# Idle products on TensorE ahead of ten waits between the stages of an eight-stage flamingo block

## What is computed

```python
x = x + tanh(g_xattn[0]) * mamba(ctx, layernorm(x))           # selective scan, 16 states
x = x + tanh(g_ffn[0])   * moe_sigmoid(layernorm(x))          # 16 experts, top 4, one shared
x = x + tanh(g_xattn[1]) * mamba(ctx, layernorm(x))
x = x + tanh(g_ffn[1])   * ternary_ffn(layernorm(x))          # weights quantised to -1, 0, 1
x = x + tanh(g_xattn[2]) * attention(layernorm(x), ctx)       # 32 heads, rotary positions
x = x + tanh(g_ffn[2])   * fp8_ffn(layernorm(x))
x = x + tanh(g_xattn[3]) * feature_attention(layernorm(x), ctx)
x = x + tanh(g_ffn[3])   * moe_softmax(layernorm(x))          # 16 experts, top 2, shared part
```

## Time and profile before

| | |
|---|---|
| median of 3 runs | 996.89 us (996.51 to 998.3) |
| profiled execution, first to last instruction | 994.6 us |
| PE busy | 824.6 us, 83% |
| DVE busy | 670.0 us, 67% |
| POOL, ACT busy | 419.8 us (42%), 406.1 us (41%) |
| mean granted TensorE clock | 0.893 of full speed |

### The profile page before, as it was taken

The page is one execution under the profiler, slowest core; times in us unless marked ns, Lnnn a source line. Parts: engine busy times, 40 slices in busy tenths (PEclk is TensorE's granted clock), DMA queues, the critical chain, the costliest instruction groups (busy, mean ns, idle before and its releaser), DMA issues.

```text
span 994.6 us, 12963 instructions
## 1 busy us (share of the span) xinstructions
PE 824.6 (83%) x4202; PEld 523.7 (53%) x4202; DVE 670.0 (67%) x1145; ACT 406.1 (41%) x832; POOL 419.8 (42%) x313
## 2 busy tenths in 40 slices
PE   7968898756899888888399779999948988979992
PEld 3323333344677767665377535555525776546651
DVE  5989999697889888889565556778727365412222
ACT  5742333253344444443354725665523432113331
POOL 3036666113575766665169402425501341423331
PEclk9979988756999999999599889999978996979997
DMA  5121214381221221220200121332144010161114
GB/s 216 48 84 67 81 64 181 157 271 52 85 85 50 78 84 42 84 84 0 75 0 1 54 64 50 100 114 76 49 144 135 1 58 7 48 202 48 44 48 153
DMA packets 28531, 81.68 MB, mean 82 GB/s; under 512 B 3360, under 2 KB 17200, under 8 KB 27088
## 3 DMA queue, kind: packets, MB, share of 16 engines
q1 hardware_dynamic: 26080, 73.25, 21.5%
q0 software_dynamic: 2256, 6.18, 1.7%
q10 hardware_dynamic: 144, 1.57, 0.4%
HBM read 65.64 MB, written 17.35 MB: 83 GB/s over the span
## 4 chain that ended last, share of the span: by engine, by line
PE 46%; issue 21%; DVE 17%; POOL 9%; DMA 3%; ACT 2%; SPq 0%; DVEq 0%; POOLq 0%; ACTq 0%
PE ps L522 5%; POOL M L689 5%; PE ps L1357 5%; PE ps L1727 4%; PE ps L1731 4%; PE ps L513 3%; PE ps L1769 3%; PE ps L396 3%; PE ps L911 3%; POOL ZT L994 2%; DVE M L658 2%; PE ps L1376 2%; DVE M L666 2%; PE ps L799 2%; PE ps L1642 1%
## 5 line engine op out<-in xcount | busy, mean ns | idle before, releaser
L799 PE MATMUL ps<-W,F 128*128 128x256 f32 x544 | 151.9, 404 | 34.8 <-DVE W L867 21.7
L799 PEld LDWEIGHTS ps<-W,F 128*128 128x128 f32 x544 | 102.2, 198 | 67.6 <-DVE W L867 40.9
L600 POOL TENSOR_TENSOR M<-M 128x1024 f32<-128x1024 f32 x32 | 75.4, 2356 | 86.1 <-DVE M L474 47.4
L696 POOL TENSOR_TENSOR W<-W,M 128x1024 f32<-128x1024 f32 x32 | 75.4, 2357 | 84.4 <-DVE M L666 84.4
L1798 ACT ACTIVATE N<-ps 128x512 f32<-128x512 f32 x128 | 69.5, 594 | 75.7 <-PE ps L1731 75.7
L831 ACT ACTIVATE F<-ps 128x128 f32<-128x128 f32 x136 | 37.8, 278 | 140.0 <-PE ps L799 140.0
L658 DVE TENSOR_TENSOR_SCAN M<-ps,M 128x512 f32<-128x512 f32 x64 | 78.0, 1219 | 21.5 <-POOL M L689 21.5
L1819 DVE TENSOR_REDUCE W<-ps 128x4 f32<-128x1024 f32 x64 | 78.1, 1221 | 8.9 <-PE ps L1731 5.9
L786 PE MATMUL ps<-W,F 128*128 128x256 f32 x272 | 83.3, 389 | 0.0
L1727 PE MATMUL ps<-M,W 32*128 32x256 f32 x512 | 74.1, 418 | 10.8 <-DVE W L1825 5.7
L616 DVE TENSOR_TENSOR_SCAN M<-ps,M 128x1024 f32<-128x1024 f32 x32 | 73.3, 2291 | 10.3 <-ACT ps L569 10.1
(11 more groups left out here) (281 smaller groups left out, 1708.8 us busy)
## 6 DMA issues: line engine op xcount, KB each, us to landing
M<-dbl_scratch SPq DMA_DIRECT2D x48, 512.0 KB, 3.7
W<-in_gu SPq DMA_DIRECT2D x1, 4800.0 KB, 16.3
W<-in_gu SPq DMA_DIRECT2D x1, 4352.0 KB, 13.9
att_scratch<-W SPq DMA_DIRECT2D x32, 128.0 KB
slot_scratch<-in_slots SPq DMA_DIRECT2D x1, 3999.0 KB, 18.7
M<-slot_scratch SPq DMA_DIRECT2D x3, 1032.0 KB, 9.6
W<-in_gu SPq DMA_DIRECT2D x2, 1536.0 KB, 6.7
W<-in_dn SPq DMA_DIRECT2D x1, 2176.0 KB, 18.6
```

What stands on the lines that cost most here:

```text
L600: nc.gpsimd.tensor_tensor(dBu[:, t, :], du[0][:, t, :], Bb[:, par, :], ALU.mult).then_inc(S("dBu_rdy"), 1)
L696: nc.gpsimd.tensor_tensor(u[1][:, t, :], u[1][:, t, :], hC[:, t, :], ALU.add).then_inc(S("y1_acc"), 1)
L799: last = nc.tensor.matmul(up, ztt[:, par, c, :], gu[:, c, s, :], start=(c == 0), stop=(c == DC - 1))
```

## The change

A helper issues `n` matmuls of `ident` by the first 512 columns of `ctxT` into a bank whose contents nobody reads any more and which the next user overwrites. They wait for nothing, count up nothing, and stand in TensorE's program at ten places, 69 in all: 5, 4, 4, 14, 13, 4, 2, 15, 3 and 5.

```diff
+        def stay_busy(bank, n, width=HALF):
+
+            for _ in range(n):
+                nc.tensor.matmul(ps[:, bank, 0:width], ident[:], ctxT[:, 0:width], start=True, stop=True)
+
@@ experts_tensor
             pe.wait_ge(S("x_done"), 4 * NT)
             pe.wait_ge(S("expert_of"), 1)
+            stay_busy(0, 5)
             turn_rows(0)
@@ the tensor block
             mamba0_tensor(pe)
+            stay_busy(6, 5)
             mamba_tail_tensor(pe, 0)
+            stay_busy(3, 4)
             ln_tensor(pe, 1, 0)
+            stay_busy(3, 4)
             pe.wait_ge(S("ld_w0"), 80)
             router_tensor(pe, 0)
+            stay_busy(3, 14)
             ffn_tensor(pe, 0)
             pe.wait_ge(S("x_done"), NT)
+            stay_busy(2, 13)
             mamba_tail_tensor(pe, 1)
+            stay_busy(3, 4)
             pe.wait_ge(S("xm_done"), 2 * BATCH)
             ternary_tensor(pe)
+            stay_busy(7, 2)
             pe.wait_ge(S("w1_rdy"), 6)
             ln_tensor(pe, 3, 1)
...
             attn2_tensor(pe)
+            stay_busy(3, 15)
             attn2_out_tensor(pe)
...
             attn3_tensor(pe)
+            stay_busy(1, 3)
             ln_tensor(pe, 7, 5)
```

## The result

The changed kernel took 988.87 us (median of 17 executions, 982.72 to 994.84), the kernel before on the same chip 996.45 (17 executions, 987.89 to 1001.55): ratio 0.9919, 95% interval 0.9897 to 0.9941. So it is faster by 7.6 us, where I had forecast 2.6 less and a range that began at 989.3. The two intervals overlap narrowly. In microseconds the first reaches from 5.9 to 10.3 gained and the second from 2.7 to 6.9, so both lie above the 2.55 of my sum. The profiled execution has a span of 987.6 us (994.6 before).

A forecast was written before the change was run, and what follows sets the result against it. PE held 46% of the chain, and after long idle waits its clock fell to 0.50. Terms 0 + 1.75 + 1.8 + 2.3 - 3.3 = 2.55 us less than 996.89 gave 994.3 us, range 989.3 to 998.8.

The forecast's parts named there:

- Price of a product: Each idle product of 512 columns makes two records: 0.86 us at full clock, some 1.70 us at half clock.
- Ahead of ffn 0, "together 0": The four runs before ffn 0 gain nothing: the run of 14 ends late, cancelling gains; bounds 1.7 gained, 3.0 lost.
- the first place: First wait behind mamba 0, 5 products: 0.6 us reaches the chain, then is swallowed by the run ahead of ffn 0.
- My upper bound, everything at full clock: For the four runs before ffn 0: 0.6 + 1.1 = 1.7 us gained if all ran at full clock.
- Behind ffn 0, 1.75: Runs of 13, 4 and 2: gains of 0.6 at L540, 0.4 at L1497, 0.75 at L334; bounds 0 and 3.
- Behind attention 2, 1.8: Run of 15 fits the idle time; L1853's first half then runs at full clock, gaining 1.8 us; bounds 0 and 1.8.
- Behind attention 3, 2.3: Run of 3 gains 2.3 us: 1.0 from the transposes plus half the router's saving, since the router lets the clock fall.
- Ahead of the experts, 3.3 lost: Five products start behind a late x_done, delaying PE likely 6.2 us; 2.2 comes back from the experts' faster start.
- the first rival: The last run costs nothing because x_done comes on time: sum 5.85, time 991.0 us; chance 0.27.
- Overrun: Half-clock products outlast their waits ahead of ffn 0 and the experts: 3.7 us slower, 1000.6 us; chance 0.11.
- Products that don't hold the clock: The idle products fail to hold full clock, so the long runs overrun: some 36 us more, 1033 us; chance 0.04.
- transposes that don't count: Transposes let the clock fall behind the runs, so 1.75 us less is gained behind ffn 0: 996.1 us; chance 0.05.

The follow-up runs named there:

- e9: The changed kernel run again, unaltered, against the kernel before (the second series): 992.07 us, ratio 0.9952.
- e1: The changed kernel without its last run, the 5 products at the start of the experts: 992.24 us, 0.9929 to the kernel before.
- e5: The changed kernel with the last five products placed before the waits for x_done and expert_of instead of behind them: 986.69 us, 0.9886.
- e8: The kernel before with only the four runs before ffn 0 (5, 4, 4 and 14 products): 994.06 us, 0.9974.
- e11: e5 plus four more products in the idle time ahead of attention 2: 982.68 us, 0.9857 to the kernel before.
- e12: e11 with longer runs: 6, 6, 4, 16 products before ffn 0 and 6 ahead of the ternary block: 986.63 us, 0.9887.
- e7: The kernel before with only the runs behind ffn 0 (13, 4, 2), attention 2 (15) and attention 3 (3): 992.03 us, 0.9951.
- e6: e5 with four runs lengthened: 6, 6, 4, 18 products before ffn 0 and 6 ahead of the ternary block: 987.96 us, 0.9902.
- e2: The kernel before with only the last run, five products behind x_done and expert_of: 999.9 us, 1.0027.
- e3: The changed kernel with three products of 16 columns in place of each product of 512: 1013.92 us, 1.0171 to the kernel before.
- e4: The changed kernel with six transposes of 128 columns in place of each product: 996.13 us, 0.9978 to the kernel before.

## Why the prediction was wrong

The direction was right, and the mechanism: wide products in the idle time hold the clock, and the work behind them runs at 1.00. Forecast 994.3, measured 988.87, or 992.07 in the second series; the range held the second and missed the first by 0.4 us. The step that failed is the zero for the four runs ahead of ffn 0; the runs showed 0.7 to 1.7 us there. In the profile of the first series the loss at the last run failed as well: 2.5 us gained in place of 3.3 lost, but in e9 the loss was there. Point by point:

- **Price of a product.** Right: at full clock the records start 0.43 us apart, 0.86 us for two (the ten at 193.17 take 4.45 us with the end of the last), and 0.85 apart at half clock.
- **Ahead of ffn 0, "together 0".** This step failed. I let the first router fall to half clock, the run of 14 begin there, take 15.0 us and end at 234.9, behind the release. In the trace the router began at full clock and the run behind it began at 217.46 instead of 219.9, though mamba 0 had ended 1.6 us later in this execution. The low spell lasted only 3.4 us, not the 6.1 that I had taken from one rise; the run took 13.82 us and ended 3.35 us early. So nothing of the first place was swallowed: from mamba 0's end to L804 it took 41.3 us, 42.0 before, close to the 0.6 that I had allowed at L540. The rest hangs on where the clock falls in the first unit of ffn 0: nothing in two profiles (the changed kernel's and e1), 1.0 us in e5, e8, e9, e11 and e12. Together the four runs bring 0.7 us in the first two and 1.6 or 1.7 in the five others, and 2.6 (0.4 to 4.7) by the times of e8. My upper bound, everything at full clock, was 1.7.
- **Behind ffn 0, 1.75.** Measured 2.2 (31.7 to 29.5): 0.6 at L540 and 0.4 at L1497, as forecast, and 1.1 at L334 in place of 0.75; mis-sized by less than half a microsecond.
- **Behind attention 2, 1.8.** Right: 11.4 to 9.6, in every profile with these products but e11 (10.5, where the run ended 2.0 us early).
- **Behind attention 3, 2.3.** Right in kind. Up to the shared expert it is 1.3 to 2.6 us in the profiles with these products, but 0.1 in e7 (14.6), where the clock fell at 834.9, before the router's first product at 836.78. Taken together with the shared expert behind it, it is 3.0 in the changed kernel, e6, e9, e11 and e12, 1.3 in e1 and e5, and 0.1 in e7. The clock falls in the router, as forecast: at 835.0 in the changed kernel, where it takes 5.57 us instead of 7.01.
- **Ahead of the experts, 3.3 lost.** Right in kind where x_done is late, with two terms off. The delay was 5.6 us in e2 and 6.8 in e9 (forecast 6.2 behind the slots). What comes back is 3.7, not 2.2: I had counted the tiles at 2.88 us apart, their later pace, but at full clock the first ones come 2.23 us apart, because the later products of an expert do not yet stand between them. That makes a net loss of 1.9 to 3.1. In the first profile x_done was on time, the delay 1.3 us and the net 2.5 gained: the first rival, just as it was written, in one of fourteen profiles.
- **The rivals.** Overrun: seen in e3 and e6, not in the changed kernel ahead of ffn 0. Products that don't hold the clock, and transposes that don't count: both refuted (the changed kernel, e4). The second I had given 0.05 from rows 3, and e4 bore that out.

With the profile of e9 the edited places sum to 1.6 + 2.2 + 1.8 + 1.9 - 3.1 = 4.4 us, and the shared expert's 34.8 us became 33.7, 1.1 more, a continued gain of the router's place: 5.5 us, between the two series (8.1 and 4.8 us by their ratios). My sum of 2.55 lacked 1.6 of it before ffn 0, 0.45 behind it, 0.7 from attention 3 through the shared expert, and 0.2 at the last run. With the first profile, where x_done was on time, the same places sum to 0.7 + 2.2 + 1.8 + 2.0 + 2.5 and 1.0 in the shared expert, 10.2 us. How often x_done is on time outside the profiles is not known, so it stays open how much of the 7.6 us of the first series is that and how much is scatter. The stages that the change does not touch scatter as well: mamba 0 took 184.0 to 187.8 us, wide stage 1 64.1 to 67.6, attention 2 141.6 to 145.9 (without e11), and the time that the clock is low in them differs too.

## What to carry to other kernels

Where a stage begins slowly behind a wait, look at the granted clock before looking for a late engine; here wide products into a bank that nobody reads held it, where they began at once behind the last work and ended close to the release. Put them ahead of the wait and not behind it: by the ratios the same five products lost 2.7 us behind x_done and gained 2.3 ahead of it. Size them for the clock they will really have: the five took 4.5 us in e5 and 7.1 in e9, where they began in a low spell, and the run lengthened to 18 products overran its release by 1.6 us.

## What the runs showed of the hardware that I had not expected

- PE can be busy throughout at either clock: 22.00 of 22.00 us with products of 16 columns at 0.50 (e3), 9.20 of 9.20 us with transposes of 128 columns at 1.00 (e4).
- The same kernel differs by 12 us between executions (982.72 to 994.84). In the two profiles of the changed kernel mamba 0 took 187.8 and 184.0 us. Attention 2 follows its time at the low clock: 141.7 us with 10.3, 143.4 with 15.3, 145.5 with 20.5.
- DVE's update behind the shared expert is released 2.8 to 2.9 us behind PE's last product in thirteen of fourteen profiles, by no instruction that the profile names. It was not found out why.
